# An image-normalising prologue ahead of a bidirectional GRU: the image loop dealt out anew among the engines

## The chip, the cores and the metric

The kernel runs on one core of one Trainium2 chip. The metric is the device time of one execution in microseconds (us). The engines of the core are TensorE (PE in the rows, with its weight loads listed apart as PEld), VectorE (DVE), ScalarE (ACT), GpSimd (POOL) and SyncE (SP), which issues every DMA of this kernel.

## What is computed

The input `x` holds 16 images of 32 x 32 tokens with 128 channels, in float32. The reference, cut to what matters:

```python
mu = x.mean(-1, keepdims=True)
var = ((x - mu) ** 2).mean(-1, keepdims=True)
xn = (x - mu) / jnp.sqrt(var + 1e-05) * ln_gamma + ln_beta
gray = xn.mean(-1)[:, None]                     # one number per token
scores = ...                                    # from gradients of gray, 4 per image
probs = jax.nn.softmax(relu(scores @ mlp_w1.T + mlp_b1) @ mlp_w2.T + mlp_b2)
idx = jnp.argmax(probs, axis=-1)
seq = jnp.where((idx == 1)[:, None, None], seq_v, seq_h)   # columns or rows of xn, 1024 tokens
z = seq @ in_w.T + in_b
yf = _gru_dir(z @ gru_wih_f.T + gru_bih_f, gru_whh_f, gru_bhh_f, False)
yb = _gru_dir(z @ gru_wih_b.T + gru_bih_b, gru_whh_b, gru_bhh_b, True)
y = jnp.concatenate([yf, yb], axis=-1) @ out_w.T + out_b
return x + y.reshape(Bx, Hx, Wx, C)
```

So each image is normalised over its channels, a gray value per token decides whether its tokens are read by rows or by columns, and then a GRU with 128 hidden units runs over 1024 steps in both directions.

## The kernel before

The work has three stages. The **image loop** goes over the 16 images. Of each it makes the normalised values, turns them so that channels lie on partitions, writes them twice into SBUF (`seq` in row order, `big`, seen as `seq_v`, in column order), and sums the channels of every token into `gray`. The **tail of the prologue** computes the gradients of `gray`, the scores and the choice per image, and replaces the first tokens of the images that are read by columns. The **recurrence** then runs 1024 steps of both directions; projections and outputs are computed between its steps.

An image lies in SBUF as 128 partitions of 8 tokens (`TPP` = 8) of 128 channels. `xin` has four slots (`SLOTS`), and image n uses slot n modulo 4. The engines work through their own instruction lists in order and wait for each other with semaphores. For image n:

- SP (`load_image`, line 306) waits until image n - 4 has been summed and turned, and issues one DMA of 512 KB (line 310). The 16 DMAs of weights and biases go out in four groups behind images 4 to 7 (lines 332 to 336); four small ones that are needed first go out behind images 0 and 1 (line 316).
- VectorE (`statistics`, line 756) makes eight statistics and eight aggregations; `scales` (line 768) makes the reciprocal of the deviation and, in `shift`, minus the mean times it.
- ScalarE (`deviation`, line 422) takes the square root between the two. It also normalises tokens 0 and 1 of the eight in place (line 432, `JA` = 2) and copies the turned image out of PSUM twice (`evacuate_rows`, line 437; `evacuate_columns`, line 443).
- GpSimd (`normalise`, line 383) normalises the other six tokens, as x * rstd + shift. It begins only when the first four parameters have landed (line 391).
- TensorE (`transposes`, line 533) turns the eight groups of 128 x 128 into one of two PSUM pairs.
- The gray sums are shared. VectorE (`gray_sums`, line 778) multiplies a token's channels by gamma and accumulates, one instruction per token and a short read of the accumulator. For the first 13 images (`N_PE`) the last three tokens (`J_PE` = 3) are summed on TensorE instead (`gray_columns`, line 542): the tokens of `seq` are the weights, taken at every eighth element, and a column of ones is streamed. A float32 product of this kind is two weight loads and two matmuls, and the result is one column of `bank[4]`. Line 803 moves these columns into `gray`, less the sum of beta.

TensorE's order in an iteration n is: transposes of n, gray columns of n - 2, then the weight products. These (`products`, line 550; `folded`, line 554) combine the input weights with the GRU's: a product per iteration 8 to 11, the folded biases in iterations 12 and 13. ScalarE takes the squared norm of the recurrent weights at n = 10 and its root at n = 13. VectorE makes a power of two of it (lines 812 to 818), behind the last gray sums; ScalarE scales and splits the weights after the loop (lines 475 to 482), VectorE makes the middle part of the split (line 841), and GpSimd adds up the biases (lines 404 to 417).

The tail begins with TensorE's halo products (line 592), which wait for all gray sums (lines 590 and 591).

Of the kernel before, what the change touches and what calls it, by code (L numbers as in the profile page):

```python
# [20 lines left out]
P = 128  # L21
# [12 lines left out]
JA = 2  # L34
J_PE = 3
N_PE = 13
# [84 lines left out]
def build(nc, x, gamma, beta, w1t, b1, w2t, b2, in_w, in_b, wiht, whht, bih, bhh, outwt, out_b, consts, out):  # L121
# [18 lines left out]
    shift = sb("shift", [P, SLOTS, TPP])  # L140
# [69 lines left out]
    w_in = sem("w_in")  # L210
    first_in = sem("first_in")
# [5 lines left out]
    shift_set = sem("shift_set")  # L217
    xhat_act = sem("xhat_act")
    xhat_pool = sem("xhat_pool")
    gray_sum = sem("gray_sum")  # L220
    select_rest = sem("select_rest")
# [58 lines left out]
    N_PARAM = 16  # L280
    N_FIRST = 4

# [20 lines left out]
    @block.sync  # L303
    def _(sp):

        def load_image(n):
            if n >= SLOTS:
                sp.wait_ge(gray_sum, n + (1 - SLOTS))
                sp.wait_ge(xT_set, n + (1 - SLOTS))
            sp.dma_start(xin[:, n % SLOTS].rearrange("p j c -> p (j c)"), x_part[n]).then_inc(x_in[n % SLOTS], 16)  # L310

        load_image(0)
        load_image(1)
        for dst, src in ((con[:, 0:P], consts[:, 0:P]), (gb[:, 0:1], gamma), (gb[:, 1:2], beta),
                         (gamma_row[:, :], gamma.rearrange("c a -> a c").to_broadcast((P, C)))):
            sp.dma_start(dst, src).then_inc(first_in, 16)
        load_image(2)
        load_image(3)
        params = (
            (inw[:, :, :], in_w.rearrange("(k p) c -> p k c", p=P)),  # L320
            (inb[:, :], in_b),
            (wih[:, 0], wiht[0].rearrange("(k p) m -> p k m", p=P)),
            (wih[:, 1], wiht[1].rearrange("(k p) m -> p k m", p=P)),
            (whh[:, 0], whht[0]), (whh[:, 1], whht[1]),
            (outw[:, 0], outwt[0:HID]), (outw[:, 1], outwt[HID:2 * HID]),
            (mlp1[:, :], w1t), (mlpb1[:, :], b1), (mlp2[:, :], w2t),
            (mlpb2[:, :], b2.to_broadcast((P, 4))),
            (bih_col[:, :, :], bih), (bhh_col[:, :, :], bhh), (bias_col[:, 8:9], out_b),
            (con[:, P:C_END], consts[:, P:C_END]),
        )  # L330
# [38 lines left out]
    def _(g):  # L369
# [51 lines left out]
    def _(act):  # L421
# [6 lines left out]
        def normalise(n):  # L428
            q = n % SLOTS
            act.wait_ge(shift_set, n + 1)  # L430
            for j in range(JA):
                ins = act.activation(xin[:, q, j, :], xin[:, q, j, :], ACT.Identity,
                                     bias=shift[:, q, j:j + 1], scale=rstd[:, q, j:j + 1])
            ins.then_inc(xhat_act, 1)


# [13 lines left out]
        deviation(0)  # L450
        act.wait_ge(first_in, 16 * N_FIRST)
        for n in range(B):
# [7 lines left out]
            if n == 10:  # L460
                act.wait_ge(w_in, 16 * N_PARAM)
                act.activation(square[:, :], whh[:, :, :].rearrange("p d n -> p (d n)"), ACT.Square,
                               accum_out=sums[:, 0:1]).then_inc(square_set, 1)
            if n == 13:
                act.wait_ge(norm_mm, 1)
                act.activation(norm[:, 0:1], bank[5][:, 4 * B:4 * B + 1], ACT.Sqrt).then_inc(norm_set, 1)
            if n == 14:
# [4 lines left out]
        evacuate_rows(B - 1)  # L472
        evacuate_columns(B - 1)

        act.wait_ge(scale_set, 1)
        w_all = whh[:, :, :].rearrange("p d n -> p (d n)")
        parts = [wsplit[:, k].rearrange("p d n -> p (d n)") for k in range(3)]
        act.activation(parts[0], w_all, ACT.Identity, scale=sk[:, 0:1]).then_inc(high_set, 1)
        act.activation(parts[2], w_all, ACT.Identity, scale=sk[:, 1:2]).then_inc(weights_set, 1)
        for d in range(2):  # L480
            act.activation(wcomb[:, d, :], bank[6 + d][:, 0:3 * HID], ACT.Identity,
                           scale=sk[:, 0:1]).then_inc(fold_set, 1)
# [43 lines left out]
    def _(pe):  # L526
# [6 lines left out]
        def transposes(n):  # L533
            pe.wait_ge(xhat_pool, n + 1)
            pe.wait_ge(xhat_act, n + 1)
            if n >= 2:
                pe.wait_ge(seq_set, 2 * n - 2)
            for j in range(TPP):
                ins = nc.tensor.transpose(pair[n % 2][:, j * P:(j + 1) * P], xin[:, n % SLOTS, j, :], identity)  # L539
# [22 lines left out]
        for n in range(B):  # L562
# [6 lines left out]
            if n == 8:  # L569
                pe.wait_ge(w_in, 16 * N_PARAM)  # L570
            if 8 <= n < 12:
                products((n - 8) // 2, n % 2)
            if n == 12:
                pe.wait_ge(square_set, 1)
                one(bank[5][:, 4 * B:4 * B + 1], ones[:, :], sums[:, :]).then_inc(norm_mm, 1)
                for g in range(3):
                    folded(0, g)
            if n == 13:
                for g in range(3):
                    ins = folded(1, g)  # L580
                ins.then_inc(w_mm, 1)
# [7 lines left out]

        pe.wait_ge(gray_sum, B)  # L590
# [151 lines left out]
    def _(dve):  # L742
# [25 lines left out]
        def scales(n):  # L768
            q = n % SLOTS
            dve.wait_ge(std_set, n + 1)  # L770
            v.reciprocal(rstd[:, q, :], std[:, q, :]).then_inc(rstd_set, 1)
            dve.wait_ge(rstd_set, n + 1)
            dve.wait_ge(moments_set, n + 1)
            v.scalar_tensor_tensor(out=shift[:, q, :], in0=moments[:, q, :, 0], scalar=-1.0, in1=rstd[:, q, :],  # L774
                                   op0=ALU.mult, op1=ALU.mult).then_inc(shift_set, 1)


        def gray_sums(n):
            dve.wait_ge(xhat_act, n + 1)
            dve.wait_ge(xhat_pool, n + 1)  # L780
            if n > 0:
                dve.wait_ge(gray_sum, n)
            for j in range(TPP - J_PE if n < N_PE else TPP):
# [3 lines left out]

        statistics(0)
# [12 lines left out]
        dve.wait_ge(gray_mm, N_PE)  # L801
# [4 lines left out]
        gray_sums(B - 1)  # L806
# [3 lines left out]


        dve.wait_ge(norm_set, 1)
        link(v.tensor_scalar(norm[:, 0:1], norm[:, 0:1], NORM_MIN, None, ALU.max))
        link(v.tensor_scalar(norm[:, 1:2].bitcast(I32), norm[:, 0:1].bitcast(I32), 0x7F800000, None, ALU.bitwise_and))
        v.tensor_scalar(scale[:, 0:1], norm[:, 1:2], 1.0 / TOP, None, ALU.mult)
        link(v.tensor_scalar(scale[:, 1:2], norm[:, 1:2], -1.0 / TOP, None, ALU.mult))
        v.reciprocal(sk[:, :], scale[:, :])
        v.tensor_scalar(usual[:, :], norm[0:1, 1:2], NORM_MIN, None, ALU.is_le).then_inc(scale_set, 1)
# [178 lines left out]
```

## Time and profile before

| | us |
|---|---|
| median of three runs | 1680.24 (1679.62 to 1682.0) |
| the profiled execution, its own time | 1683.49 |
| its span, first to last instruction | 1681.7 |
| image loop, to the first halo product | 73.1 |
| tail of the prologue, to the first step | 14.77 |
| recurrence | 1593.83 |

The engines' shares of the span are TensorE 96%, its weight loads 73%, VectorE 86%, ScalarE 69% and GpSimd 3%. They are almost all of the recurrence; the change is in the first 88 us, so its stretches have to be read by themselves. In the rows, a line of the order of time gives the start, the time from the start of the first to the end of the last instruction in a group, the engine, the line of the code, the operation, output and input with their shapes, the count, and in brackets the idle time before it and what ended that. Instructions overlap: the next begins before the last has ended, so that the distance between two starts tells what an instruction costs its engine.

### The profile page before, as it was taken

Reading aid. Unit: us, or ns where it says so; the run is one execution under the profiler, and the core shown is the slowest. Engines: PE = TensorE matmul, PEld = TensorE weight load, DVE = VectorE, ACT = ScalarE, POOL = GpSimd, SP = SyncE. Lnnn points to the kernel's source line nnn. Section 1 sums busy time; section 2 is a strip of 40 time slices with the busy share of each in tenths; the row PEclk is TensorE's granted clock in tenths of the full one; section 3 lists DMA queues with packets and bytes.
Section 4 is the critical chain, followed back from the end, with each engine's and each line's share of the span. In section 5 each row is a group of like instructions: output and inputs, shape, how many; then the busy total and the mean of one; then the engine's idle time right before and its main releaser. Section 6 shows DMA issues by size and latency. Waiting matters only on the chain.

```text
span 1681.7 us, 61485 instructions
## 1 busy us (share of the span) xinstructions
PE 1612.0 (96%) x21687; PEld 1230.9 (73%) x21687; DVE 1450.3 (86%) x9046; ACT 1162.8 (69%) x6241; POOL 49.6 (3%) x123
## 2 busy tenths in 40 slices
PE   5899999999999999999999999999999999999997
PEld 5777777777777777777777777777777777777775
DVE  7889999888888888888888888888888888888887
ACT  6866666666666666666666666666666666666666
POOL 5500000000000000000000000000000000000000
PEclk9755555555555555555555555555555555555555
DMA  5200000000000000000000000000000000000000
GB/s 179 74 12 15 12 15 12 12 15 12 13 13 12 14 12 12 14 12 15 12 12 8 12 15 12 14 14 12 15 12 14 13 12 14 13 13 13 12 13 17
DMA packets 40360, 31.29 MB, mean 19 GB/s; under 512 B 3576, under 2 KB 37880, under 8 KB 40056
## 3 DMA queue, kind: packets, MB, share of 16 engines
q1 hardware_dynamic: 40056, 27.35, 5.6%
q8 instruction: 177, 2.90, 0.7%
q14 instruction: 127, 1.04, 0.2%
HBM read 18.95 MB, written 8.39 MB: 16 GB/s over the span
## 4 chain that ended last, share of the span: by engine, by line
DVE 69%; ACT 21%; issue 7%; DMA 1%; PE 1%; POOL 0%; SPq 0%; DVEq 0%
DVE state L904 30%; ACT drive L509 20%; DVE bank L893 18%; DVE halves L913 12%; DVE big L885 3%; DVE seq L869 2%; DVE xin L885 1%; DVE stats L760 1%; DMA xin<-in_x 1%; DVE drive L920 1%; DVE weighted L784 0%; POOL xin L387 0%; DMA gamma_row<-in_gamma 0%; DVE moments L764 0%; PE bank L539 0%
## 5 line engine op out<-in xcount | busy, mean ns | idle before, releaser
L627 PEld LDWEIGHTS bank<-halves,wsplit 128*128 128x128 f16 x18432 | 653.6, 106 | 393.9 <-DVE halves L913 287.3
L627 PE MATMUL bank<-halves,wsplit 128*128 128x16 f16 x18432 | 839.5, 181 | 39.9 <-DVE halves L913 36.4
L904 DVE TENSOR_TENSOR_SCAN state<-gain,drive 128x48 f32<-128x48 f32 x2048 | 526.1, 257 | 172.1 <-ACT drive L509 40.9
L627 PE MATMUL bank<-seq,wcomb 128*128 128x128 f32 x1536 | 592.9, 482 | 2.2 <-DVE seq L869 2.2
L509 ACT ACTIVATE drive<-bank 128x16 f32<-128x16 f32 x2048 | 396.1, 193 | 270.0 <-DVE bank L893 2.2
L503 ACT ACTIVATE rpair<-bank 128x16 f32<-128x16 f32 x2048 | 381.0, 186 | 221.5 <-PE bank L627 221.5
L893 DVE TENSOR_TENSOR_SCAN bank<-rpair,bank 128x32 f32<-128x32 f32 x2048 | 454.4, 222 | 3.4 <-ACT rpair L503 3.4
L913 DVE SCALAR_TENSOR_TENSOR halves<-state 128x32 f16<-128x32 f32 x2048 | 398.4, 195 | 35.5
L506 ACT ACTIVATE gain<-bank 128x16 f32<-128x16 f32 x2048 | 394.2, 192 | 0.0
L627 PEld LDWEIGHTS bank<-seq,wcomb 128*128 128x128 f32 x1536 | 386.0, 311 | 2.7 <-DVE seq L869 2.7
L920 DVE SCALAR_TENSOR_TENSOR drive<-gain,state 128x16 f32<-128x16 f32 x2046 | 364.8, 178 | 0.0
L627 PE MATMUL bank<-ind,bias 6*128 6x128 bf16 (+1 forms) x768 | 297.9, 390 | 0.0
L627 PE MATMUL bank<-outw,state 128*128 128x128 f32 x512 | 197.9, 491 | 0.9 <-DVE state L904 0.9
L627 PEld LDWEIGHTS bank<-outw,state 128*128 128x128 f32 x512 | 128.7, 310 | 1.0 <-DVE state L904 1.0
L627 PEld LDWEIGHTS bank<-ind,bias 6*128 6x128 bf16 x768 | 75.8, 99 | 18.0
L885 DVE TENSOR_TENSOR big<-bank,big 128x128 f32<-128x128 f32 x192 | 54.4, 283 | 0.0
L539 PE MATMUL bank<-con,xin 128*128 128x128 f32 x128 | 28.0, 391 | 21.8 <-POOL xin L387 21.8
L387 POOL TENSOR_SCALAR xin<-xin,rstd,shift 128x128 f32<-128x128 f32 x96 | 45.9, 497 | 23.4 <-DVE shift L774 16.3
L539 PEld LDWEIGHTS bank<-con,xin 128*128 128x128 f32 x128 | 22.8, 206 | 25.1 <-POOL xin L387 12.7
L869 DVE COPY_PREDICATED seq<-mask,big 128x160 f32<-128x160 int32 (+2 forms) x98 | 38.6, 395 | 0.0
L627 PE MATMUL bank<-obias,ones 3*128 3x128 bf16 x128 | 36.2, 283 | 0.0
L760 DVE BATCH_NORM_STATS2 stats<-xin 128x6 f32<-128x128 f32 x128 | 26.2, 278 | 7.9 <-DMA xin<-in_x 6.4
(100 smaller groups left out, 222.0 us busy)
## 6 DMA issues: line engine op xcount, KB each, us to landing
xin<-in_x SPq DMA_DIRECT2D x16, 512.0 KB, 3.6
big<-in_x SPq DMA_DIRECT2D x96, 64.0 KB
out<-big SPq DMA_DIRECT2D x96, 64.0 KB
xin<-in_x SPq DMA_DIRECT2D x32, 64.0 KB
out<-xin SPq DMA_DIRECT2D x32, 64.0 KB
wih<-in_wiht SPq DMA_DIRECT2D x2, 384.0 KB
con<-in_consts SPq DMA_DIRECT2D x1, 572.0 KB
whh<-in_whht SPq DMA_DIRECT2D x2, 192.0 KB
```

The source lines that it names most:

```text
L387: ins = g.tensor_scalar(xin[:, q, j, :], xin[:, q, j, :], rstd[:, q, j:j + 1], shift[:, q, j:j + 1], ALU.mult, ALU.add)
L503: act.activation(rpair[:, e, 2 * B * d:2 * B * (d + 1)].rearrange("p (n k) -> p n k", k=2)[:, :, 1], R[q][:, at:at + B], ACT.Sigmoid, scal ...
L506: act.activation(thirds_of(gain, e, d)[:, :, 1], Z[q][:, at:at + B], ACT.Sigmoid, scale=negative).then_inc(update_ready[d], 1)
L509: act.activation(thirds_of(drive, e, d)[:, :, 0], candidate_of(q, e, d).rearrange("p (n k) -> p n k", k=2)[:, :, 1], ACT.Tanh, scale=negat ...
L539: ins = nc.tensor.transpose(pair[n % 2][:, j * P:(j + 1) * P], xin[:, n % SLOTS, j, :], identity)
L627: return nc.tensor.matmul(o, w, m, start=start, stop=True, skip_group_check=True)
L869: return v.copy_predicated(seq[:, :, t0:t1], mask[:, :].unsqueeze(2).to_broadcast([P, B, t1 - t0]), seq_v[:, :, t0:t1])
L885: v.tensor_tensor(t, Y[j % 2][:, d * C:(d + 1) * C], t, ALU.add).then_inc(y_used, 1)
L893: v.tensor_tensor_scan(candidate_of(q, e, d), rpair[:, e, 2 * B * d:2 * B * (d + 1)], NX[q][d][:, at:at + 2 * B], 0.0, ALU.mult, ALU.add). ...
L904: v.tensor_tensor_scan(state[:, d, ring, :], gain[:, e, cols], drive[:, e, cols], 0.0, ALU.mult, ALU.subtract).then_inc(state_ready[d], 1)
L913: v.scalar_tensor_tensor(out=halves[:, e, d, :, :], in0=new[:, :, 2].unsqueeze(1).to_broadcast([P, 2, B]), scalar=-BIG, in1=both, op0=ALU. ...
L920: v.scalar_tensor_tensor(out=thirds_of(drive, e, d)[:, :, 1], in0=thirds_of(gain, e, d)[:, :, 1], scalar=-1.0, in1=old[:, :, 1], op0=ALU.a ...
```

## The change

- **Channel sums.** `J_PE` becomes 7 and `N_PE` 14: for images 0 to 13 TensorE sums seven of the eight tokens, VectorE one. For image 14 VectorE sums all eight, and for image 15 it sums the raw values less their mean and multiplies by the reciprocal deviation at the end (`raw_gray_sums`).
- **Normalisation.** `shift` is gone. A normalisation is (x - mean) * rstd, with two scalars per partition. VectorE does tokens 0 and 1 in place of ScalarE, GpSimd the other six, without the wait for the first parameters. Image 15 is written to slot 0 rather than in place, so that its raw values stay.
- **Deviations.** ScalarE makes two deviations ahead of the loop, and in iteration n that of image n + 2, between the two copies of image n (before: of image n + 1, between the copies of image n - 1).
- **Weights.** The input weights are issued behind the first parameters and ahead of images 2 and 3, the recurrent weights behind image 3; ten other transfers go out one by one behind images 6 to 15. The products move to iterations 0 and 1 (four matmuls per iteration, behind a wait for these weights), the folded biases to 2 and 3, the norm to 6. ScalarE's and VectorE's work on the weights moves into the loop. TensorE waits for the remaining parameters behind the loop.

The core of the diff:

```diff
-JA = 2
-J_PE = 3
-N_PE = 13
+JD = 2
+J_PE = 7
+N_PE = 14
...
+    def xhat_slot(n):
+
+        return n % SLOTS if n < B - 1 else (n + 1) % SLOTS
...
+        for dst, src in ((inw[:, :, :], in_w.rearrange("(k p) c -> p k c", p=P)), (inb[:, :], in_b),
+                         (wih[:, 0], wiht[0].rearrange("(k p) m -> p k m", p=P)),
+                         (wih[:, 1], wiht[1].rearrange("(k p) m -> p k m", p=P))):
+            sp.dma_start(dst, src).then_inc(proj_in, 16)
         load_image(2)
         load_image(3)
+        for d in range(2):
+            sp.dma_start(whh[:, d], whht[d]).then_inc(whh_in, 16)
...
         for n in range(SLOTS, B):
             load_image(n)
-            if n < 2 * SLOTS:
-                for dst, src in params[(n - SLOTS) * 4:(n - SLOTS + 1) * 4]:
+            if n >= SLOTS + 2:
+                for dst, src in params[(n - SLOTS) - 2:(n - SLOTS) - 1]:
                     sp.dma_start(dst, src).then_inc(w_in, 16)
...
         def normalise(n):
-            q = n % SLOTS
-            g.wait_ge(shift_set, n + 1)
-            for j in range(JA, TPP):
-                ins = g.tensor_scalar(xin[:, q, j, :], xin[:, q, j, :], rstd[:, q, j:j + 1], shift[:, q, j:j + 1],
-                                      ALU.mult, ALU.add)
+            q, to = n % SLOTS, xhat_slot(n)
+            g.wait_ge(rstd_set, n + 1)
+            if to != q:
+                g.wait_ge(xT_set, n + (2 - SLOTS))
+            for j in range(JD, TPP):
+                ins = g.tensor_scalar(xin[:, to, j, :], xin[:, q, j, :], moments[:, q, j, 0:1], rstd[:, q, j:j + 1],
+                                      ALU.subtract, ALU.mult)
             ins.then_inc(xhat_pool, 1)
 
-        g.wait_ge(first_in, 16 * N_FIRST)
...
         for n in range(B):
-            normalise(n)
-            if n > 0:
-                evacuate_rows(n - 1)
-            if n < B - 1:
-                deviation(n + 1)
-            if n > 0:
-                evacuate_columns(n - 1)
...
+            evacuate_rows(n)
+            if n + 2 < B:
+                deviation(n + 2)
+            evacuate_columns(n)
+            if n == 4:
+                act.wait_ge(whh_in, 16 * N_REC)
+                act.activation(square[:, :], w_all, ACT.Square, accum_out=sums[:, 0:1]).then_inc(square_set, 1)
...
+            if n == 11:
+                act.wait_ge(scale_set, 1)
+                act.activation(parts[0], w_all, ACT.Identity, scale=sk[:, 0:1]).then_inc(high_set, 1)
+            if n == 12:
+                act.activation(parts[2], w_all, ACT.Identity, scale=sk[:, 1:2]).then_inc(weights_set, 1)
...
             if 2 <= n < N_PE + 2:
                 gray_columns(n - 2)
-            if n == 8:
-                pe.wait_ge(w_in, 16 * N_PARAM)
-            if 8 <= n < 12:
-                products((n - 8) // 2, n % 2)
-            if n == 12:
+            if n < 2:
+                pe.wait_ge(proj_in, 16 * N_PROJ)
+                for k in range(DI // P):
+                    products(n, k)
+            if 2 <= n < 4:
+                for g in range(3):
+                    ins = folded(n - 2, g)
+                if n == 3:
+                    ins.then_inc(w_mm, 1)
+            if n == 6:
                 pe.wait_ge(square_set, 1)
                 one(bank[5][:, 4 * B:4 * B + 1], ones[:, :], sums[:, :]).then_inc(norm_mm, 1)
...
+        pe.wait_ge(w_in, 16 * N_PARAM)
         pe.wait_ge(gray_sum, B)
         pe.wait_ge(gray_set, 1)
...
+            for j in range(JD):
+                ins = v.tensor_scalar(xin[:, to, j, :], xin[:, q, j, :], moments[:, q, j, 0:1], rstd[:, q, j:j + 1],
+                                      ALU.subtract, ALU.mult)
+            ins.then_inc(xhat_dve, 1)
...
         statistics(0)
         scales(0)
+        normalise(0)
         dve.wait_ge(first_in, 16 * N_FIRST)
         for n in range(B):
             if n < B - 1:
                 statistics(n + 1)
-            if n > 0:
-                gray_sums(n - 1)
-            if n < B - 1:
+                gray_sums(n)
                 scales(n + 1)
+                normalise(n + 1)
...
+            if n == 10:
+                weight_scale()
+        raw_gray_sums(B - 1)
         dve.wait_ge(gray_mm, N_PE)
         dve.wait_ge(beta_set, 1)
         v.tensor_scalar(gray[:, 0:N_PE, TPP - J_PE + 1:TPP + 1],
```

## Rows read from the trace of the kernel before

**Rows 1.** Busy time (instructions) by stage: stretch, length, five engines, granted clock, DMA, GB/s.

```profile
11.67:47.00 35.33, 26.16 (x117) 25.17 (x117) 31.65 (x246) 28.66 (x43) 24.89 (x54) 1.00 0.57 177
47.00:63.20 16.20, 15.39 (x82) 13.19 (x83) 15.61 (x121) 14.90 (x25) 12.15 (x25) 1.00 0.41 131
63.20:73.10 9.90, 9.71 (x48) 9.29 (x46) 8.37 (x69) 6.97 (x13) 6.78 (x15) 0.52 0.01 2
73.10:87.87 14.77, 11.32 (x89) 9.07 (x89) 8.16 (x34) 8.64 (x12) 1.91 (x8) 0.50 0.03 9
87.87:1681.70 1593.83, 1549.43 (x21359) 1174.14 (x21357) 1381.27 (x8542) 1100.66 (x6144) 0.00 (x0) 0.50 0.05 13
```

**Rows 2.** The chain that ended last, at the loop's end: start, length, work.

```profile
73.16 1.85 PE bank L531 x8
```

**Rows 3.** TensorE's weight loads in order of time, 43.5 to 61 us.

```profile
43.94 1.57 PEld L539 LDWEIGHTS bank<-con,xin 128*128 128x128 f32 x8 [1.80 <-POOL xin L387]
45.49 1.53 PEld L531 LDWEIGHTS bank<-ones,seq 128*128 128x128 f32 x6
46.92 0.52 PEld L551 LDWEIGHTS bank<-wih,inw 128*128 128x128 f32 x2
...
55.13 0.85 PEld L539 LDWEIGHTS bank<-con,xin 128*128 128x128 f32 x8 [0.56 <-POOL xin L387]
55.96 1.50 PEld L531 LDWEIGHTS bank<-ones,seq 128*128 128x128 f32 x6
57.36 0.32 PEld L551 LDWEIGHTS bank<-wih,inw 128*128 128x128 f32 x2
```

**Rows 4.** The same view, 57 to 75 us.

```profile
61.58 1.42 PEld L556 LDWEIGHTS bank<-inb,wih 128*128 128x128 f32 x12
62.83 1.00 PEld L539 LDWEIGHTS bank<-con,xin 128*128 128x128 f32 x8
...
65.25 2.66 PEld L556 LDWEIGHTS bank<-inb,wih 128*128 128x128 f32 x12
67.65 1.76 PEld L539 LDWEIGHTS bank<-con,xin 128*128 128x128 f32 x8
69.39 1.53 PEld L531 LDWEIGHTS bank<-ones,seq 128*128 128x128 f32 x6
```

**Rows 5.** TensorE's matmuls in order of time: two pairs of weight products.

```profile
46.97 1.63 PE L551 MATMUL bank<-wih,inw 128*128 128x384 f32 x2
...
51.36 0.89 PE L551 MATMUL bank<-wih,inw 128*128 128x384 f32 x2
```

**Rows 6.** VectorE in order of time: the first scales, and one image's period.

```profile
6.98 0.20 DVE L771 RECIPROCAL rstd<-std 128x8 f32<-128x8 f32 x1 [0.37 <-ACT std L425]
...
44.48 1.64 DVE L760 BATCH_NORM_STATS2 stats<-xin 128x6 f32<-128x128 f32 x8
...
46.71 0.27 DVE L784 SCALAR_TENSOR_TENSOR weighted<-xin,gamma_row 128x128 f32<-128x128 f32 x1
46.90 0.08 DVE L784 DVE_READ_ACCUMULATOR weighted<-xin,gamma_row 128x1 f32 x1
...
48.14 1.64 DVE L760 BATCH_NORM_STATS2 stats<-xin 128x6 f32<-128x128 f32 x8
```

**Rows 7.** GpSimd in order of time: the first and a later image.

```profile
8.96 2.61 POOL L387 TENSOR_SCALAR xin<-xin,rstd,shift 128x128 f32<-128x128 f32 x6 [7.15 <-DMA gamma_row<-in_gamma]
...
44.66 2.90 POOL L387 TENSOR_SCALAR xin<-xin,rstd,shift 128x128 f32<-128x128 f32 x6 [0.77 <-DVE shift L774]
```

**Rows 8.** ScalarE in order of time: a row copy and the deviation behind it.

```profile
45.95 1.20 ACT L439 ACTIVATE seq<-bank,gb 128x1024 f32<-128x1024 f32 x1 [0.48 <-PE bank L539]
47.05 0.29 ACT L425 ACTIVATE std<-moments,eps 128x8 f32<-128x8 f32 x1
```

**Rows 9.** SP's issues in order of time: the last of the first parameters.

```profile
3.05 0.43 SPq L316 DMA_DIRECT2D gamma_row<-in_gamma  x1
```

**Rows 10.** The tile `xin`: how long its loads took to land.

```profile
DMA to landing us min/median/max: 3.3/3.6/7.4
```

More of the change, by code:

```diff
@@ L139, in build @@
     rstd = sb("rstd", [P, SLOTS, TPP])
-    shift = sb("shift", [P, SLOTS, TPP])
     gamma_row = sb("gamma_row", [P, C])
@@ L210, in build @@
     w_in = sem("w_in")
+    proj_in = sem("proj_in")
+    whh_in = sem("whh_in")
     first_in = sem("first_in")
@@ L216, in build @@
     rstd_set = sem("rstd_set")
-    shift_set = sem("shift_set")
-    xhat_act = sem("xhat_act")
+    xhat_dve = sem("xhat_dve")
     xhat_pool = sem("xhat_pool")
     gray_sum = sem("gray_sum")
+    raw_gray = sem("raw_gray")
     select_rest = sem("select_rest")
@@ L278, in build @@
     x_part = x_tok.rearrange("b (p j) c -> b p (j c)", j=TPP)
-    N_PARAM = 16
+    N_PARAM = 10
+    N_PROJ = 4
+    N_REC = 2
     N_FIRST = 4
+    def xhat_slot(n):
+        return n % SLOTS if n < B - 1 else (n + 1) % SLOTS
     def place(s, d):
@@ L425, in deviation @@
             act.activation(std[:, q, :], moments[:, q, :, 1], ACT.Sqrt, bias=eps[:, 0:1]).then_inc(std_set, 1)
[L428 to L434, printed above, removed]
         def evacuate_rows(n):
@@ L450, in _ @@
         deviation(0)
+        deviation(1)
         act.wait_ge(first_in, 16 * N_FIRST)
+        w_all = whh[:, :, :].rearrange("p d n -> p (d n)")
+        parts = [wsplit[:, k].rearrange("p d n -> p (d n)") for k in range(3)]
         for n in range(B):
-            normalise(n)
-            if n > 0:
-                evacuate_rows(n - 1)
-            if n < B - 1:
-                deviation(n + 1)
-            if n > 0:
-                evacuate_columns(n - 1)
[L460 to L467, printed above, removed]
+            evacuate_rows(n)
[5 more added lines that the diff above has]
+                act.activation(square[:, :], w_all, ACT.Square, accum_out=sums[:, 0:1]).then_inc(square_set, 1)
+            if n == 5:
                 act.wait_ge(w_mm, 1)
@@ L471, in _ @@
                 ins.then_inc(fold_set, 1)
[L472 to L482, printed above, removed]
+            if n == 7:
+                act.wait_ge(norm_mm, 1)
+                act.activation(norm[:, 0:1], bank[5][:, 4 * B:4 * B + 1], ACT.Sqrt).then_inc(norm_set, 1)
+            if n == 11:
[3 more added lines that the diff above has]
+                act.activation(parts[2], w_all, ACT.Identity, scale=sk[:, 1:2]).then_inc(weights_set, 1)
+            if n == 13:
+                for d in range(2):
+                    act.activation(wcomb[:, d, :], bank[6 + d][:, 0:3 * HID], ACT.Identity,
+                                   scale=sk[:, 0:1]).then_inc(fold_set, 1)
         act.wait_ge(bias_mm, 1)
@@ L538, in transposes @@
             for j in range(TPP):
-                ins = nc.tensor.transpose(pair[n % 2][:, j * P:(j + 1) * P], xin[:, n % SLOTS, j, :], identity)
+                ins = nc.tensor.transpose(pair[n % 2][:, j * P:(j + 1) * P], xin[:, xhat_slot(n), j, :], identity)
             ins.then_inc(xT_set, 1)
@@ L771, in scales, with normalise @@
             v.reciprocal(rstd[:, q, :], std[:, q, :]).then_inc(rstd_set, 1)
+        def normalise(n):
+            q, to = n % SLOTS, xhat_slot(n)
             dve.wait_ge(rstd_set, n + 1)
             dve.wait_ge(moments_set, n + 1)
-            v.scalar_tensor_tensor(out=shift[:, q, :], in0=moments[:, q, :, 0], scalar=-1.0, in1=rstd[:, q, :],
-                                   op0=ALU.mult, op1=ALU.mult).then_inc(shift_set, 1)
+            if to != q:
+                dve.wait_ge(xT_set, n + (2 - SLOTS))
+            for j in range(JD):
+                ins = v.tensor_scalar(xin[:, to, j, :], xin[:, q, j, :], moments[:, q, j, 0:1], rstd[:, q, j:j + 1],
+                                      ALU.subtract, ALU.mult)
+            ins.then_inc(xhat_dve, 1)
         def gray_sums(n):
-            dve.wait_ge(xhat_act, n + 1)
-            dve.wait_ge(xhat_pool, n + 1)
+            own = TPP - J_PE if n < N_PE else TPP
+            dve.wait_ge(xhat_dve, n + 1)
+            if own > JD:
+                dve.wait_ge(xhat_pool, n + 1)
             if n > 0:
                 dve.wait_ge(gray_sum, n)
-            for j in range(TPP - J_PE if n < N_PE else TPP):
+            for j in range(own):
                 ins = v.scalar_tensor_tensor(out=weighted[:, j, :], in0=xin[:, n % SLOTS, j, :], scalar=1.0, in1=gamma_row[:, :],
@@ L786, in gray_sums, with raw_gray_sums, weight_scale @@
             ins.then_inc(gray_sum, 1)
+        def raw_gray_sums(n):
+            q = n % SLOTS
+            dve.wait_ge(gray_sum, n)
+            for j in range(TPP):
+                ins = v.scalar_tensor_tensor(out=weighted[:, j, :], in0=xin[:, q, j, :], scalar=moments[:, q, j, 0:1],
+                                             in1=gamma_row[:, :], op0=ALU.subtract, op1=ALU.mult,
+                                             accum_out=gray[:, n, 1 + j:2 + j])
+            ins.then_inc(raw_gray, 1)
+            dve.wait_ge(raw_gray, 1)
+            v.tensor_tensor(gray[:, n, 1:TPP + 1], gray[:, n, 1:TPP + 1], rstd[:, q, :], ALU.mult).then_inc(gray_sum, 1)
+        def weight_scale():
+            dve.wait_ge(norm_set, 1)
+            link(v.tensor_scalar(norm[:, 0:1], norm[:, 0:1], NORM_MIN, None, ALU.max))
+            link(v.tensor_scalar(norm[:, 1:2].bitcast(I32), norm[:, 0:1].bitcast(I32), 0x7F800000, None, ALU.bitwise_and))
+            v.tensor_scalar(scale[:, 0:1], norm[:, 1:2], 1.0 / TOP, None, ALU.mult)
+            link(v.tensor_scalar(scale[:, 1:2], norm[:, 1:2], -1.0 / TOP, None, ALU.mult))
+            v.reciprocal(sk[:, :], scale[:, :])
+            v.tensor_scalar(usual[:, :], norm[0:1, 1:2], NORM_MIN, None, ALU.is_le).then_inc(scale_set, 1)
         statistics(0)
         scales(0)
+        normalise(0)
         dve.wait_ge(first_in, 16 * N_FIRST)
```

23 lines of the change are left out of this document (2 added, 21 removed).

## The prediction

> **What bounds the kernel now.** I read the stages first, the busy time of each engine in each stretch. The recurrence, from the first step at 87.87 us to the end, is 1593.83 of the 1681.70 us, and the change touches no instruction of it [rows 1]. At stake is the prologue: the image loop up to 73.1 us, and a tail of 14.77 us between the loop and the first step, in which no engine is busy throughout and one matrix product, copy or comparison waits for the last [rows 1]. The chain of waits confirms where the tail begins: TensorE's halo products at 73.16 us [rows 2]. A microsecond won or lost before that moves the whole recurrence by as much.
>
> Then I read the loop engine by engine, one image each. VectorE begins the statistics of one image at 44.48 us and of the next at 48.14 us, a period of 3.66 us; 2.23 us of it (44.48 to 46.71) are the statistics, the rest five channel sums and the scales [rows 6]. TensorE loads the weights of eight transposes in 1.55 us (43.94 to 45.49) and those of three channel sums in 1.43 us (45.49 to 46.92): each float32 sum is two passes, so six loads of 0.238 us [rows 3]. That is 2.98 us of TensorE in a period of 3.66: **VectorE is the bound, and TensorE has only 0.7 us left per image.** GpSimd's six normalisations take 2.90 us [rows 7]; ScalarE's row copy holds it for 1.10 us, and the column copy about as long [rows 8].
>
> The clock of TensorE has to be read from durations. The granted clock is shown as 1.00 up to 63.2 us and as 0.50 after [rows 1]. But eight transpose loads took 1.55 us at 43.94 and 0.83 us (55.13 to 55.96) later [rows 3], a factor of about two: 1.2 GHz first, 2.4 GHz while the weight products were in the loop, and 1.74 us (67.65 to 69.39) again after the fall [rows 4]. The sums' loads did not follow: six took 1.43 us at the low clock and 1.40 us (55.96 to 57.36) at the high one [rows 3]. They take every eighth element of a row of `seq`. The loads of the folded biases, which read neighbouring elements, did halve, from 2.40 us (65.25 to 67.65) to 1.25 us (61.58 to 62.83) for twelve [rows 4].
>
> **The change, part by part.**
>
> *VectorE.* Out go four of five channel sums and the shift, in come two normalisations. A sum costs VectorE about 0.21 us: the five sums and the scales fill 46.71 to 48.14, or 1.43 us, and 0.35 of that I give to the scales [rows 6]. No row shows a two-scalar operation of 128 elements on VectorE; the bounds are 0.08 us (a read of the accumulator, one element) and 0.27 us (a sum of 128 elements, run to its end) [rows 6]; I take 0.2, near the sum of the same size. New period: 2.23 + 0.21 + 0.25 + 2 x 0.2 = 3.1 us. A gain of 0.6 us per image, if VectorE still set the pace.
>
> *ScalarE* loses two normalisations per image and has about 2.4 us left; the weight work, moved into the loop, adds about 1 us in a few images. *GpSimd* keeps six of its operations, 2.90 us. Both stay below VectorE. The waits that come with it (the scale on ScalarE at image 11, the norm on VectorE at image 10, the freed slot for image 15) are for results made iterations earlier, so nothing queued behind them is held up. One chain over two images remains: scales, GpSimd 2.90, transposes about 1.9 to the end of the last (their loads alone 1.57 [rows 3]), row copy 1.10, the deviation queued behind it 0.29 [rows 8], scales 0.2 [rows 6] and some 0.3 of semaphores, together 6.7 us for two images, 3.4 each.
>
> *TensorE.* Seven sums instead of three: 14 loads x 0.238 = 3.33 us, with 1.55 of transposes **4.88 us per image at the low clock**, 0.83 + 3.33 = 4.16 at the high one. Either is above every other engine and above today's 3.66. So TensorE becomes the bound, and what VectorE saves is idle time.
>
> Now the clock time of the loop's end. *Start:* GpSimd no longer waits for the first parameters; scales(0) end at 6.98 + 0.20 [rows 6], GpSimd runs 7.3 to 9.9 (2.61 at 8.96 [rows 7]) and transposes(0) load from 9.9 to 11.5. *Weights:* four issues, 0.43 us each and a little between [rows 9], go ahead of images 2 and 3 on SP, so the last is given out by about 5.4 us. Their landing is not shown; image loads landed in 3.3 to 7.4 us, median 3.6 [rows 10], so 8.7 to 12.8 us, and TensorE wants them at 11.5. I take no wait, and 1.3 us as the upper end; behind that wait stand transposes(1), and behind those ScalarE's copies and the deviation of image 3. Images 2 and 3 slip by 1.9 us from an issue right behind that of 3.05 [rows 9], which the 4 us until VectorE wants image 2 (about 12) can take. *Products:* two pairs per direction, 1.63 us a pair at the low clock and 0.89 at the high one [rows 5]. The first two end at 14.8, as the first parameters still hold image 1 and its six normalisations until then. Transposes(1) and one small product end at 16.8; products(1) take 1.8 to 3.3 us, so iteration 2 starts at 18.6 to 20.1. *Iterations 2 to 15* carry transposes and sums: 14 x 4.88 = 68.3 us at the low clock. *Folded biases:* 24 loads in iterations 2 and 3, 4.8 us low, 2.5 high; the norm 0.4. Low clock throughout: 20.1 + 68.3 + 4.8 + 0.4 = 93.6 us. *Hand-over:* the sums of image 13 now end the loop. VectorE must copy them out before the halo products: 0.2 us to the last product's end, 0.27 us for the copy, as long as a sum [rows 6], 0.1 of semaphores. Halos at 94.2 against 73.16: **+21 us**.
>
> How long does the high clock last? It came while the first weight products ran among transposes, and was gone 5 us after the last pair: these loads were out at 57.36 and the folded loads still short at 61.58, those at 65.25 long [rows 3, 4]. With four pairs by about 18 us I expect it for products(1) (-1.5) and iteration 2 (-0.7, and -1.2 for its folded biases): -3.4. **Sum: +17.6 us.**
>
> *Tail.* The weight preparation that leaves it was beside the chain: nothing on the chain waits for it. The split that does stand in it stays where it was. I cost it at zero; the cover of the rest is VectorE's own sequence. The parameters, now one per image, end with the constants at image 15, three iterations before the halos need them. The recurrence: zero.
>
> The profiled execution took 1683.49 us, 3.25 above the median of the runs (1680.24) and above the highest. Its own time would become 1701.1; the median, 1697.8. What a measurement can tell from no change is about 0.2%, 3.4 us.
>
> **The rivals.**
>
> *A: TensorE rises to 2.4 GHz and stays there*, because it now never idles. Iteration 2 from 18.6, 14 x 4.16 = 58.2, folded 2.5, norm 0.3, hand-over 0.5: 80.1, so +6.9 us, 1687.1. Against it: from 63.2 to 73.1 us TensorE was busy 9.71 of 9.90 us at a granted 0.52 [rows 1], with the same mix of transposes and one-column sums. In the Trainium skill, TensorE: Matmul & The Clock Gate, section "Why this matters for your kernels", advises keeping TensorE continuously busy without idle gaps, so that it keeps the full clock; by that rule this rival would be the forecast. The stretch just named disagrees with it. Chance 0.13.
>
> *B: faster, because a one-column sum costs less than its load*, the loads being hidden under one another or under the transposes once there are fourteen in a row. If a load came down to 0.104 us (1.25/12 [rows 4]), TensorE would need 0.83 + 1.46 and the two-image chain would set 3.4 us: 18.6 + 13 x 3.4 + 1.55 + 1.5 + 0.5 = 66.4, so -6.8 us, 1673.4. It decides at the load where the loop ends as now: (73.16 - 0.5 - 5.2 - 18.6)/14 = 3.49 per iteration, less 1.55, over 14: 0.139 us. For it: TensorE's load queue works ahead of the products. Against it: six in a row already ran at 0.234 to 0.238 at either clock [rows 3]. Chance 0.05; that it lands within 0.2% on the way, 0.03.
>
> *C: slower still*, TensorE waiting for GpSimd in every image on top of its own work. A normalisation slowed by VectorE's new operations beside it would have to take the two-image chain from 6.7 beyond 9.8 us, half as much again. Above 1703; chance 0.05.
>
> **How the numbers follow.** Forecast 0.74, A 0.13, B 0.05, no change 0.03, C 0.05. The forecast with its bounds (+17.6 to +21, weights 1.3 late) reaches 1697.8 to 1702.5. The range takes in A: 1686 to 1703. Faster 0.05, within 0.2% 0.03, slower 0.92.
>
> **What would show it.** After: TensorE's weight loads without idle time from about 15 us to the halos; 14 loads of a sum in 3.3 us; eight transposes in 1.55 us for most images; VectorE and GpSimd idle more than 1.5 us per image; halo products at 90 to 94 us; the tail 14.8 and the recurrence 1594 us as before. Wrong if the 14 loads take under 2 us, if transposes take 0.83 us to the end (A), or if halos come before 73 us (B).

## The result, and the profile after

The changed kernel takes **1703.8 us** in the median of four runs (1703.35 to 1704.21) against 1680.01 before: 1.0139 of the time, with a 95% interval of 1.0122 to 1.0157. It is slower by 23.8 us, as forecast in kind, but beyond the range (1686 to 1703) and a third more than the +17.6 forecast.

Busy time by stage in the changed kernel, with columns as in [rows 1]: up to the first transposes, iterations 0 and 1, iterations 2 to 4, iterations 5 to 14 as far as the last one's sums, the rest of the loop up to the halo products, the tail, the recurrence.

```profile
0.00:12.15 12.15, 0.00 (x0) 0.00 (x0) 6.97 (x45) 2.09 (x4) 6.10 (x23) 1.00 0.83 279
12.15:21.59 9.44, 7.71 (x26) 5.11 (x26) 6.85 (x46) 4.98 (x6) 9.44 (x13) 1.00 0.37 128
21.59:40.47 18.88, 18.88 (x90) 18.88 (x91) 9.38 (x64) 7.66 (x10) 15.28 (x20) 0.59 0.24 84
40.47:86.82 46.35, 46.35 (x209) 46.35 (x210) 31.16 (x211) 25.79 (x36) 42.54 (x54) 0.50 0.30 96
86.82:96.73 9.91, 8.58 (x38) 8.41 (x38) 2.72 (x18) 4.60 (x4) 6.71 (x17) 0.50 0.01 2
96.73:111.19 14.46, 10.36 (x88) 8.45 (x89) 7.58 (x28) 3.76 (x6) 0.00 (x0) 0.62 0.03 8
111.19:1702.40 1591.21, 1547.01 (x21359) 1168.97 (x21357) 1384.10 (x8542) 1097.02 (x6144) 0.00 (x0) 0.50 0.05 13
```

The loop ends at 96.73 us in place of 73.1, 23.6 later, which is the whole loss; the tail is 0.3 us shorter. From 21.59 to 86.82 us TensorE has no idle time at all. But the last of the engines' columns surprises: GpSimd is busy 42.54 of 46.35 us there, where the prediction had given it 2.9 us of every 4.9.

TensorE's weight loads in order of time show one iteration, then the end of the loop; they answer to [rows 3].

```profile
21.59 0.86 PEld L538 LDWEIGHTS bank<-con,xin 128*128 128x128 f32 x8 [2.16 <-POOL xin L397]
22.42 3.40 PEld L530 LDWEIGHTS bank<-ones,seq 128*128 128x128 f32 x14
25.72 2.66 PEld L555 LDWEIGHTS bank<-inb,wih 128*128 128x128 f32 x12
28.12 1.76 PEld L538 LDWEIGHTS bank<-con,xin 128*128 128x128 f32 x8
...
40.47 1.78 PEld L538 LDWEIGHTS bank<-con,xin 128*128 128x128 f32 x8
42.23 3.43 PEld L530 LDWEIGHTS bank<-ones,seq 128*128 128x128 f32 x14
45.38 1.78 PEld L538 LDWEIGHTS bank<-con,xin 128*128 128x128 f32 x8
...
91.19 1.57 PEld L538 LDWEIGHTS bank<-con,xin 128*128 128x128 f32 x8 [0.94 <-POOL xin L397]
92.74 3.43 PEld L530 LDWEIGHTS bank<-ones,seq 128*128 128x128 f32 x14
```

An image costs TensorE 4.91 us (40.47 to 45.38), 1.76 of it transposes and 3.15 the fourteen loads; 4.88 had been forecast. The brackets tell the rest: both iteration 2 and the last transposes wait for GpSimd. Its operations in order of time, answering to [rows 7]:

```profile
7.33 23.84 POOL L397 TENSOR_SCALAR xin<-xin,moments,rstd 128x128 f32<-128x128 f32 x30 [5.52 <-DVE rstd L770]
...
79.19 4.75 POOL L397 TENSOR_SCALAR xin<-xin,moments,rstd 128x128 f32<-128x128 f32 x6 [0.16 <-DVE rstd L770]
86.03 5.10 POOL L397 TENSOR_SCALAR xin<-xin,moments,rstd 128x128 f32<-128x128 f32 x6 [2.09 <-DVE rstd L770]
```

Six normalisations take 4.75 us, not 2.90. GpSimd runs without a pause from 7.33 us over five images, so that image 2 is ready after 18 operations, at 21.55. TensorE's loads for the products of iteration 1 end at 19.43 and then wait 2.16 us for it; the forecast had iteration 2 begin at 18.6.

### The profile page after: what moved, and what is told of

It is laid out like the page before. It is cut to its first block, busy times and chain, and to the rows that moved or that the text cites. A ratio compares the mean times of both kernels' runs of the same rounds, so it can differ in the third digit from the quotient of the medians.

```text
span 1702.4 us, 61586 instructions
## 1 busy us (share of the span) xinstructions
PE 1638.9 (96%) x21805; PEld 1256.2 (74%) x21805; DVE 1448.8 (85%) x8945; ACT 1145.9 (67%) x6209; POOL 80.1 (5%) x123
## 4 chain that ended last, share of the span: by engine, by line
DVE 67%; ACT 20%; issue 7%; PE 4%; POOL 2%; DMA 0%; DVEq 0%; POOLq 0%
DVE state L925 30%; ACT drive L508 20%; DVE bank L914 17%; DVE halves L934 12%; DVE big L906 3%; PE bank L530 2%; DVE seq L890 2%; POOL xin L397 2%; PE bank L538 1%; DVE xin L906 1%; DVE drive L941 1%; PE bank L555 0%; PE bank L626 0%; DMA xin<-in_x 0%; DVE stats L759 0%
## 5 line engine op out<-in xcount | busy, mean ns | idle before, releaser
L397 POOL TENSOR_SCALAR xin<-xin,moments,rstd 128x128 f32<-128x128 f32 x96 | 76.4, 810 | 12.9 <-DVE rstd L770 12.9
L530 PEld LDWEIGHTS bank<-ones,seq 128*128 128x128 f32 x196 | 48.0, 335 | 0.0
L439 ACT ACTIVATE seq<-bank,gb 128x1024 f32<-128x1024 f32 x16 | 19.3, 1206 | 42.0 <-PE bank L538 42.0
L530 PE MATMUL bank<-ones,seq 128*128 128x1 f32 x196 | 46.3, 365 | 0.0
L538 PEld LDWEIGHTS bank<-con,xin 128*128 128x128 f32 x128 | 26.8, 237 | 16.6 <-issue 12.2
```

The lines of the kernel that those rows point to most:

```text
L397: ins = g.tensor_scalar(xin[:, to, j, :], xin[:, q, j, :], moments[:, q, j, 0:1], rstd[:, q, j:j + 1], ALU.subtract, ALU.mult)
L530: return nc.tensor.matmul(out, w, m, start=start, stop=True, skip_group_check=True)
```

## The experiments

Three theories were to be told apart. The first: TensorE's seven sums set the loop's pace, and GpSimd costs only the late start. The second: GpSimd's new normalisation sets it, and TensorE follows. The third: both stand at nearly the same height, so that either alone is enough (the expectation of after_three_columns calls this one theory 2). Times are compared with the kernel before on the same chip. It took 1680.01 us beside the changed kernel, 1681.04 beside after_pool_muladd and after_three_columns, 1682.53 beside the next four rows and 1680.56 beside the last two. "Halo" is the start of the halo products, the loop's end, in the profiled execution alone; executions of one kernel differ by 1 to 7 us, so the times can differ by a few microseconds more or less than the halos.

| kernel | median us | against before | halo, us |
|---|---|---|---|
| before | 1680.01 | | 73.16 |
| changed | 1703.8 | 1.0139 (1.0122 to 1.0157) | 96.76 |
| after_pool_muladd | 1701.92 | 1.0120 (1.0103 to 1.0137) | 92.05 |
| after_three_columns | 1697.9 | 1.0098 (1.0081 to 1.0115) | 90.84 |
| after_both | 1681.34 | 0.9990 (0.9981 to 1.0000) | 73.21 |
| before_seven_sums | 1709.77 | 1.0160 (1.0145 to 1.0176) | 99.64 |
| before_pool_submul | 1698.26 | 1.0095 (1.0079 to 1.0110) | 88.49 |
| early_weights_four_sums | 1683.08 | 1.0006 (0.9997 to 1.0015) | 73.78 |
| sums_dense_loads | 1693.15 | 1.0078 (1.0062 to 1.0094) | 84.51 |
| spread_weights_three_sums | 1676.91 | 0.9979 (0.9970 to 0.9988) | 71.50 |

**What makes GpSimd slow** (pool_forms, on the kernel before):

```diff
-                ins = g.tensor_scalar(xin[:, q, j, :], xin[:, q, j, :], rstd[:, q, j:j + 1], shift[:, q, j:j + 1],
-                                      ALU.mult, ALU.add)
+                mean, r, sh = moments[:, q, j, 0:1], rstd[:, q, j:j + 1], shift[:, q, j:j + 1]
+                form = ((r, sh, ALU.mult, ALU.add), (mean, r, ALU.subtract, ALU.mult), (sh, r, ALU.subtract, ALU.mult),
+                        (sh, r, ALU.add, ALU.mult), (r, sh, ALU.mult, ALU.subtract))[min(n // 3, 4)]
+                ins = g.tensor_scalar(xin[:, q, j, :], xin[:, q, j, :], *form)
```

> The kernel before with five forms of GpSimd's normalisation, three images each (the last form four): multiply-add with rstd and shift; subtract-multiply with the mean (every second element) and rstd; subtract-multiply with shift and rstd (both dense); add-multiply with shift and rstd; multiply-subtract with rstd and shift. The values of images 3 to 15 are other than the reference's. The changed kernel took 793 ns for an operation, the one before 455 to 497. If the operation subtract makes it slow, images 3 to 8 and 12 to 15 take 0.79 us an operation and the others 0.48; if the order (multiply second) does, images 3 to 11; if the strided mean does, images 3 to 5 alone; if VectorE's own normalisations beside it did, none does. GpSimd's slow images last about 4.75 us, the others 2.9.

GpSimd's operations in that run (one execution, 1692.46 us), in order of time (three of the lines merge several images):

```profile
17.59 2.88 POOL L390 TENSOR_SCALAR xin<-xin,rstd,shift 128x128 f32<-128x128 f32 x6 [0.77 <-DVE shift L776]
21.25 14.93 POOL L390 TENSOR_SCALAR xin<-xin,moments,rstd 128x128 f32<-128x128 f32 x18 [0.77 <-DVE shift L776]
36.17 17.72 POOL L390 TENSOR_SCALAR xin<-xin,shift,rstd 128x128 f32<-128x128 f32 x24
54.84 2.89 POOL L390 TENSOR_SCALAR xin<-xin,shift,rstd 128x128 f32<-128x128 f32 x6 [0.95 <-DVE shift L776]
...
63.03 20.25 POOL L390 TENSOR_SCALAR xin<-xin,rstd,shift 128x128 f32<-128x128 f32 x24 [1.08 <-DVE shift L776]
```

Multiply-add takes 2.88 us for six, add-multiply 2.89 (the line at 54.84, two dense scalars). Subtract-multiply takes 14.93 for eighteen, or 4.98 for six, with the strided mean. With dense scalars it is as slow: the next line holds three such images and one of add-multiply, and (17.72 - 2.89)/3 is 4.94. Multiply-subtract takes 20.25/4 = 5.06. So it is the **subtraction, in either place**; the order of the operations, the stride of the mean and VectorE's new work beside it are not needed. Why a subtraction costs more there, no run shows.

**One part of the change undone at a time.** GpSimd as multiply-add again (after_pool_muladd):

```diff
+            v.scalar_tensor_tensor(out=shift[:, q, :], in0=moments[:, q, :, 0], scalar=-1.0, in1=rstd[:, q, :],
+                                   op0=ALU.mult, op1=ALU.mult).then_inc(shift_set, 1)
...
-            g.wait_ge(rstd_set, n + 1)
+            g.wait_ge(shift_set, n + 1)
...
-                ins = g.tensor_scalar(xin[:, to, j, :], xin[:, q, j, :], moments[:, q, j, 0:1], rstd[:, q, j:j + 1],
-                                      ALU.subtract, ALU.mult)
+                ins = g.tensor_scalar(xin[:, to, j, :], xin[:, q, j, :], rstd[:, q, j:j + 1], shift[:, q, j:j + 1],
+                                      ALU.mult, ALU.add)
```

> The changed kernel with GpSimd's normalisation as multiply-add again (VectorE makes the shift again), all else as changed. Theory 1, TensorE's seven sums set the pace by themselves: an image still takes 4.9 us, the gain is the faster start (iteration 2 at 18 to 20 us in place of 21.6) and the wait before the last transposes (0.9): 1699 to 1701 us. Theory 2, GpSimd's two-scalar form sets the pace and TensorE merely follows: an image falls to about 3.5 us, 1683 to 1685 us.

TensorE's transposes in that run:

```profile
17.81 1.09 PE L540 MATMUL bank<-con,xin 128*128 128x128 f32 x8 [0.52 <-POOL xin L399]
24.55 1.95 PE L540 MATMUL bank<-con,xin 128*128 128x128 f32 x8
...
57.01 1.95 PE L540 MATMUL bank<-con,xin 128*128 128x128 f32 x8
61.92 1.95 PE L540 MATMUL bank<-con,xin 128*128 128x128 f32 x8
```

1701.92 us, 0.9 above the 1699 to 1701 of theory 1; theory 2 falls. TensorE keeps 4.9 us per image; iteration 2 begins at 17.8 us and the halo products 4.7 us sooner.

Four of TensorE's seven sums left out (after_three_columns):

```diff
-            for j in range(TPP - J_PE, TPP):
+            for j in range(TPP - 3, TPP):
...
+        v.memset(bank[4][:, 0:N_PE * J_PE], 0.0)
```

> The changed kernel with four of the seven channel sums on TensorE left out (their columns of gray are then wrong), GpSimd's two-scalar form kept. Theory 1, TensorE alone is the bound: an image falls from 4.9 to about 3.5 us, 1683 to 1685 us. Theory 2, GpSimd is a second bound of nearly the same height (4.75 us an image): the pace stays at 4.75 to 4.9 us, and the gain is what TensorE's last sums and its own extra work cost at the end, 4 to 8 us: 1696 to 1700 us.

1697.9 us: theory 1 falls as well. GpSimd's line of that run, and TensorE's transposes beside it:

```profile
7.38 72.53 POOL L397 TENSOR_SCALAR xin<-xin,moments,rstd 128x128 f32<-128x128 f32 x90 [5.57 <-DVE rstd L771]
```

```profile
50.91 1.97 PE L538 MATMUL bank<-con,xin 128*128 128x128 f32 x8 [1.75 <-POOL xin L397]
55.82 1.97 PE L538 MATMUL bank<-con,xin 128*128 128x128 f32 x8 [1.74 <-POOL xin L397]
```

Fifteen images without a pause on GpSimd, 4.84 us each, and TensorE, with 1.7 us to spare, still turns one image in 4.9 us.

Both together (after_both, the two diffs above):

> The changed kernel with both: GpSimd as multiply-add and four of TensorE's seven sums left out (wrong columns of gray). If the two are equal bounds that hide each other, this one gains far more than the two single edits together: TensorE has 1.75 + 1.43 = 3.2 us per image, GpSimd 2.9, VectorE 3.4, the chain over two images 3.4 each, so the loop ends near 9.9 + 15 x 3.45 + 4 = 66 us and the halo products come at 67 to 70 us: 1674 to 1678 us. If some third thing holds the loop, it stays above 1690.

1681.34 us against 1682.53 on that chip. Undone singly, the two parts give back 4.7 and 5.9 us of loop (halo 92.05 and 90.84 from 96.76), together 23.6 (73.21): two bounds of one height. In time, each against the kernel before on its chip, it is 2.9, 6.9 and 25.0 us. It is not the 67 to 70 us that was expected. VectorE now paces the loop: its statistics of two images begin at 39.54 and 43.05 us, 3.51 apart,

```profile
39.54 1.64 DVE L762 BATCH_NORM_STATS2 stats<-xin 128x6 f32<-128x128 f32 x8
...
42.46 0.17 DVE L779 SCALAR_TENSOR_TENSOR shift<-moments,rstd 128x8 f32<-128x8 f32 x1
42.54 0.60 DVE L784 TENSOR_SCALAR xin<-xin,moments,rstd 128x128 f32<-128x128 f32 x2
43.05 1.63 DVE L762 BATCH_NORM_STATS2 stats<-xin 128x6 f32<-128x128 f32 x8
```

its two normalisations cost 0.51 us from start to start, and the eight sums of image 14, which the change puts ahead of the scales of image 15, hold up the last one: GpSimd starts on it at 66.22 us, 1.5 later than its pace would have it, and TensorE waits 2.40 us for it where it had waited 0.35.

**One part alone, on the kernel before.** Only `J_PE` = 7 and `N_PE` = 14 (before_seven_sums), and only GpSimd's form (before_pool_submul):

```diff
-J_PE = 3
-N_PE = 13
+J_PE = 7
+N_PE = 14
```

> The kernel before with only the dealing of the sums changed: seven on TensorE, for 14 images (its products stay in iterations 8 to 11, the folded biases in 12 and 13). Theory 1: 14 images at 4.9 us, the products 1.4 us each beside them and 2.4 for each folded bias set, halo products near 98 us: 1701 to 1706 us. If seven sums were harmless without the slow GpSimd form: at or under 1680.

```diff
-                ins = g.tensor_scalar(xin[:, q, j, :], xin[:, q, j, :], rstd[:, q, j:j + 1], shift[:, q, j:j + 1],
-                                      ALU.mult, ALU.add)
+                ins = g.tensor_scalar(xin[:, q, j, :], xin[:, q, j, :], moments[:, q, j, 0:1], rstd[:, q, j:j + 1],
+                                      ALU.subtract, ALU.mult)
```

> The kernel before with only GpSimd's normalisation changed, to subtract-multiply with mean and rstd (it still waits for the shift). Theory 2: GpSimd takes 4.75 us an image and paces the loop alone, 16 x 4.85 from 9 us is 86.6, transposes and halo products near 89 us: 1695 to 1697 us. If GpSimd's slower form hides behind TensorE: at 1680.

The first shows TensorE's transposes and then the halo products, the second one line of GpSimd for all 16 images:

```profile
54.10 1.91 PE L539 MATMUL bank<-con,xin 128*128 128x128 f32 x8
60.40 1.91 PE L539 MATMUL bank<-con,xin 128*128 128x128 f32 x8
...
99.64 1.89 PE L531 MATMUL bank<-gray,con 128*128 128x16 f32 x8 [2.11 <-DVE weighted L784]
```

```profile
8.97 77.49 POOL L387 TENSOR_SCALAR xin<-xin,moments,rstd 128x128 f32<-128x128 f32 x96 [7.17 <-DMA gamma_row<-in_gamma]
```

Each alone makes the kernel slower, by 27.2 and 15.7 us against 1682.53 on that chip, as the third theory has it; both are above what was expected, by 3.8 and 1.3 us. The sums alone cost more than the whole change: there the weight products stand in the full iterations 8 to 11 and lengthen them to 6.2 us and more, while the change has them before the sums begin, and TensorE waits 2.11 us ahead of the halo products for VectorE's last eight sums.

**The stride of the sums' loads** (sums_dense_loads, on after_pool_muladd):

```diff
-                ins = one(bank[4][:, at:at + 1], tokens[:, :, j], ones[:, 0:1])
+                ins = one(bank[4][:, at:at + 1], seq[:, n, j * P:(j + 1) * P], ones[:, 0:1])
```

> The kernel of after_pool_muladd (GpSimd as multiply-add, seven sums on TensorE), but each sum takes 128 neighbouring elements of a row of seq as its weights instead of every eighth (so it sums other tokens, and gray is then wrong). In the prediction the stride explained why the sums' loads took 0.238 us at either clock. If the stride is the cause, a load falls to about 0.213 us at the low clock, as the folded biases had it: 14 x 0.213 + 1.75 = 4.7 us an image in place of 4.9, 3 us less than after_pool_muladd, and 0.104 us where the clock is high. If the stride costs nothing, loads and time stay as they were.

Its weight loads, at the high and at the low clock:

```profile
18.90 1.64 PEld L532 LDWEIGHTS bank<-ones,seq 128*128 128x128 f32 x14
20.46 1.42 PEld L557 LDWEIGHTS bank<-inb,wih 128*128 128x128 f32 x12
...
29.93 3.11 PEld L532 LDWEIGHTS bank<-ones,seq 128*128 128x128 f32 x14
32.77 1.76 PEld L540 LDWEIGHTS bank<-con,xin 128*128 128x128 f32 x8
```

Fourteen dense loads take 1.56 us at the high clock (18.90 to 20.46) and 2.84 at the low one; the strided ones of the changed kernel took 3.30, about the last quarter of it at the low clock, and 3.15. So the stride is why the sums gain nothing from the clock, as argued, and it costs 0.3 us per image at the low clock. The gain of 8.8 us (1701.92 to 1693.15; 8.3 with each against the kernel before on its chip) is more than the 3 expected: about 4 are that, and 3 more come from iteration 2, which now ran at the high clock throughout, 3.75 us from transposes to transposes (18.08 to 21.83) in place of 6.74.

**The kernel before, profiled again** (before_again, no edit):

> The kernel before, unchanged, for a second profile. Its first profiled execution took 1683.49 us, 3.5 above the median, with a recurrence of 1593.83 us; the changed kernel's recurrence took 1591.21 us. If the extra time of that one execution lay in the recurrence, this profile shows a loop and a tail as before (halo products at 73.1 us, tail 14.8) and a recurrence near 1591; if the change itself shortened the recurrence, it is near 1594 again.

```profile
88.00:1678.00 1590.00, 1546.64 (x21360) 1167.91 (x21359) 1384.99 (x8542) 1096.45 (x6144) 0.00 (x0) 0.50 0.05 13
```

1680.47 us, halo at 73.49 and a recurrence of about 1590 us: the first profile's 3 extra microseconds lay in the recurrence, and the change does not touch it.

**Versions meant to beat both.** Early weights, products and folded biases in iterations 0 and 1, four sums on TensorE for 14 images (early_weights_four_sums):

```diff
-J_PE = 3
-N_PE = 13
+J_PE = 4
+N_PE = 14
...
-        g.wait_ge(first_in, 16 * N_FIRST)
...
+            if n < 2:
+                pe.wait_ge(proj_in, 16 * N_PROJ)
+                for k in range(DI // P):
+                    products(n, k)
+                for g in range(3):
+                    ins = folded(n, g)
```

> The kernel before with what should be left when both bounds are avoided: multiply-add on GpSimd and no wait for the first parameters, ScalarE's two normalisations kept, the input weights loaded early with products and folded biases in iterations 0 and 1, and four sums on TensorE for 14 images. TensorE: 1.75 + 1.9 = 3.65 us an image at the low clock, VectorE 3.45, chain over two images 3.45 each. Start 1.7 us earlier, no products in the later iterations: halo products at 66 to 70 us, 1673 to 1678 us. If TensorE's weights in the first iterations hold the loop up, no better than 1680.

```profile
13.29 1.64 DVE L761 BATCH_NORM_STATS2 stats<-xin 128x6 f32<-128x128 f32 x8 [2.85 <-DMA xin<-in_x]
73.78 1.86 PE L533 MATMUL bank<-gray,con 128*128 128x16 f32 x8 [2.11 <-DVE weighted L785]
```

No better: 1683.08 against 1682.53. With the weights issued ahead of image 2, VectorE waited 2.85 us for that image; and with sums in the last iteration VectorE's copy of TensorE's columns comes late, and its own last eight sums stand behind it, for which TensorE waits 2.11 us ahead of the halo products. These waits are read from the trace; no run removes them.

The other one (spread_weights_three_sums) leaves the sums alone, puts the weights behind image 3 and splits the last image evenly:

```diff
         load_image(2)
         load_image(3)
+        for dst, src in ((inw[:, :, :], in_w.rearrange("(k p) c -> p k c", p=P)), (inb[:, :], in_b),
+                         (wih[:, 0], wiht[0].rearrange("(k p) m -> p k m", p=P)),
+                         (wih[:, 1], wiht[1].rearrange("(k p) m -> p k m", p=P))):
+            sp.dma_start(dst, src).then_inc(proj_in, 16)
...
-            for j in range(JA, TPP):
+            for j in range(JA if n < B - 1 else 2 * JA, TPP):
...
-        g.wait_ge(first_in, 16 * N_FIRST)
```

> The kernel before with the parts of the change that take nothing from a scarce engine: no wait of GpSimd for the first parameters, the input and recurrent weights issued behind images 2 and 3 and the rest one by one behind images 6 to 15, three sums on TensorE, products where they were; and, for image 15 alone, four normalisations on ScalarE and four on GpSimd. Expected: first transposes at 10.2 in place of 11.7 us, no waits for images 4 and 7 behind weights (3.1 us before), the last transposes 0.9 us sooner: halo products at 68 to 71 us in place of 73.1, 0.998 to 0.997 of the time before. If the loop's pace of 3.66 us takes the gain back, the same time.

**1676.91 us, 0.9979 of the time before (0.9970 to 0.9988)**, the only version faster than the kernel before, with the halo products at 71.50, half a microsecond later than expected. They account for 1.7 of the 3.65 us; its profiled execution was the slowest of eleven, and no run separates what its parts bring.

## Why the prediction was right and wrong

*Right: TensorE as a bound.* Its image took 4.91 us for the 4.88 worked out. That they agree so closely is luck: the transposes took 1.76 us for 1.55 (the row of 1.57 stood behind a pause; [rows 4] has 1.74 without one), the fourteen loads 3.15 for 3.33. The tail and the recurrence stayed, as costed. VectorE's normalisations, taken as 0.2 us each between bounds of 0.08 and 0.27, took 0.25 to 0.29 and were idle time anyway.

*Wrong: "GpSimd keeps six of its operations, 2.90 us".* The change also turns multiply-add into subtract-multiply, and the prediction priced the new form by the row of the old one, without bounds: for VectorE's new operation it gave two ends, for GpSimd's none. It takes 4.75 us. So "Both stay below VectorE" failed as well: GpSimd is a second bound, 0.16 us below TensorE's, and not idle for 1.5 us per image. Rival C had named GpSimd, as a normalisation slowed by VectorE, at a chance of 0.05; pool_forms shows that the operation alone does it. The time lies where C had it, above 1703, but not by C's mechanism: TensorE does not wait for GpSimd in every image.

Of the 5.9 us between the forecast halo (90.8) and the measured one (96.73), the trace gives 3.0 to the start of iteration 2 (21.59 for 18.6) and 1.2 to the last transposes (91.19, where the loads before them, at the usual 3.15 us, end at 89.97). Both come from GpSimd's form: after_pool_muladd has neither, and gives 4.7 us of loop back. The last wait also passes through VectorE:

```profile
85.73 0.20 DVE L770 RECIPROCAL rstd<-std 128x8 f32<-128x8 f32 x1
```

GpSimd ends image 14 at 83.94 us; the change puts VectorE's eight sums of that image, which wait for it, ahead of these scales of image 15, and GpSimd stands idle for 2.09 us before that image. The folded biases of iteration 2 account for 1.15: 2.40 us (25.72 to 28.12) where 1.25 was taken, because the clock fell while that iteration's sums ran: granted 1.00 (2.4 GHz) up to 24.6 us, it was 0.50 (1.2 GHz) from 25.0 on. It was not the late start: in after_pool_muladd the iteration began 3.8 us sooner and took the same 6.74 us. The remaining 0.6 are the longer iterations and the hand-over. GpSimd's 4.75 us beside TensorE's 4.91 cost nothing in between; with TensorE relieved, in after_three_columns, it shows.

*Rival A*, the high clock kept by work without idle time, is refuted by the changed kernel itself: from 40.47 to 86.82 us TensorE is busy 46.35 of 46.35 us at a granted 0.50. The Trainium skill, TensorE: Matmul & The Clock Gate, section "Why this matters for your kernels", asks for work without gaps to keep the clock; here work without gaps, but made up mostly of weight loads for single columns, did not. *Rival B* failed as argued: fourteen loads in a row run at 0.225 us.

The size of the miss, in short: TensorE's part of the mechanism held; the sum was short mostly by one term, GpSimd's price, and beside it by the clock in iteration 2. Why TensorE, never idle, stayed at the low clock is open: no run set out to show it.

## What to carry to other kernels

An operation written another way is a new operation: price it by bounds, on each engine that gets it, even where count and shape stay. When a change loads two engines at once, taking one part back tells little; here each part alone cost 16 to 27 us, both 24, and each undone gave back a few. Before work is moved to an engine that looks idle in part, add it to that engine's own period: 0.7 us of slack do not hold 1.9 us of work.

## What the runs showed of the hardware

- On GpSimd a two-scalar operation on 128 x 128 float32 values took, in the mean of an image, 0.79 to 0.85 us if one of its operations was a subtraction and, but for the last image of the loop, 0.43 to 0.50 if they were a multiplication and an addition, in either order.
- Weight loads of 128 x 128 float32 took 0.233 us a pass with every eighth element at the high clock (1.40 us for six, [rows 3]) and 0.225 at the low one (the changed kernel); dense ones took 0.111 and 0.203 (sums_dense_loads).
